# Feature-major down products for two expert layers, weighted by broadcast routing rows and added in place

## What is computed

```python
x = x + L0_ffn(L0_cond(x, cond))      # mixtures of experts
x = x + L1_ffn(L1_cond(cond, x))      # L1_cond: a GRU over the 128 time steps
x = x + L2_ffn(L2_cond(x, v, ...))    # L2_cond: low-rank product and gelu
x = x + L3_ffn(L3_cond(x, cond))      # L3_cond: a tanh recurrence; 12 experts, 3 routers
```

```python
h = gelu(x @ W1[e] + b1[e])                   # for every expert e
out = sum_e comb[:, e] * (h @ W2[e] + b2[e])  # comb: two non-zero weights a token
```

## Time and profile before

| what | value |
|---|---|
| time of the runs | 710.54 us median (703.42 to 712.31) |
| profiled execution | 709.84 us, span 708.1 us |
| TensorE matmul (PE) | 660.8 us busy, 93% |
| TensorE weight load (PEld) | 608.8 us, 86% |
| VectorE (DVE) | 384.4 us, 54% |
| ScalarE (ACT) | 279.1 us, 39% |
| GpSimd (POOL) | 45.5 us, 6% |
| granted TensorE clock, mean | 0.964 of full |

### The profile page before, as it was taken

The page is one execution under the profiler, slowest core; times in us unless marked ns, Lnnn a source line. Parts: engine busy times, 40 slices in busy tenths (PEclk is TensorE's granted clock), DMA queues, the critical chain, the costliest instruction groups (busy, mean ns, idle before and its releaser), DMA issues.

```text
span 708.1 us, 12692 instructions
## 1 busy us (share of the span) xinstructions
PE 660.8 (93%) x4762; PEld 608.8 (86%) x4762; DVE 384.4 (54%) x1462; ACT 279.1 (39%) x930; POOL 45.5 (6%) x55
## 2 busy tenths in 40 slices
PE   5789999879999989999999999997999999999997
PEld 5678887778999978999999999997889889888895
DVE  1885757753657454455544651136555554665504
ACT  0284535533664444544454555545422112110010
POOL 3000000000001000000000000000021221221310
PEclk9999989956999999999999999999989999999999
DMA  9960000000000000000000000400000000000000
GB/s 276 391 246 1 1 1 1 2 0 1 1 2 2 1 1 2 1 1 1 1 2 1 1 1 1 151 30 0 1 1 1 5 5 1 5 5 1 7 1 9
DMA packets 18285, 20.62 MB, mean 29 GB/s; under 512 B 2900, under 2 KB 10928, under 8 KB 18224
## 3 DMA queue, kind: packets, MB, share of 16 engines
q1 hardware_dynamic: 14488, 18.76, 7.6%
q10 hardware_dynamic: 3736, 1.04, 0.6%
HBM read 19.28 MB, written 0.52 MB: 28 GB/s over the span
## 4 chain that ended last, share of the span: by engine, by line
PE 78%; DVE 11%; ACT 3%; issue 3%; DVEq 0%
PE Y L1132 29%; PE U L1132 27%; PE HH L1132 8%; PE ZR L1132 7%; PE M L1132 5%; DVE acc_b L645 1%; DVE acc_a L645 1%; DVE fresh L645 1%; PE M L1402 1%; ACT cand L501 1%; DVE h_gru L645 1%; PE U L1253 1%; DVE rh L645 1%; DVE l_up_lo L637 1%; ACT gated L525 1%
## 5 line engine op out<-in xcount | busy, mean ns | idle before, releaser
L1132 PE MATMUL Y<-l_dn,gated 128*128 128x128 f32 x1152 | 163.5, 286 | 3.7 <-DVE acc_a L827 2.1
L1132 PEld LDWEIGHTS Y<-l_dn,gated 128*128 128x128 f32 x1152 | 142.2, 194 | 6.5 <-issue 4.2
L525 ACT ACTIVATE gated<-U,b1T 128x256 f32<-128x256 f32 x256 | 106.5, 471 | 4.1 <-PE U L1132 4.1
L1132 PE MATMUL U<-l_x_hi,l_up_hi 128*128 128x256 f32 x256 | 84.1, 328 | 0.0
L505 ACT ACTIVATE h<-ZR,rnn_b 128x8 f32<-128x8 f32 x128 | 34.2, 267 | 117.4 <-PE ZR L1132 114.3
L1132 PE MATMUL U<-l_x_lo,l_up_hi 128*128 128x256 f32 x256 | 73.1, 285 | 0.0
L1132 PE MATMUL U<-l_x_hi,l_up_lo 128*128 128x256 f32 x256 | 72.9, 285 | 0.0
L501 ACT ACTIVATE cand<-HH 128x8 f32<-128x8 f32 x128 | 22.7, 177 | 122.6 <-PE HH L1132 122.6
L645 DVE SCALAR_TENSOR_TENSOR fresh<-zr_s,cand 128x8 f32<-128x8 f32 x128 | 22.7, 177 | 70.4 <-ACT cand L501 69.4
L1132 PEld LDWEIGHTS HH<-rh,gru_u 128*128 128x128 f32 x256 | 42.4, 199 | 20.4 <-DVE rh L645 19.3
L1132 PE MATMUL U<-scaled_hi,l_up_hi 128*128 128x256 f32 x192 | 58.7, 306 | 0.0
(11 more groups left out here) (270 smaller groups left out, 1265.1 us busy)
## 6 DMA issues: line engine op xcount, KB each, us to landing
w_raw<-L_ffn_W_dram SPq DMA_DIRECT2D x1, 3072.0 KB, 10.9
l_up_raw<-L_ffn_W_dram SPq DMA_DIRECT2D x1, 2048.0 KB, 14.3
l_up_raw<-L_ffn_w_dram SPq DMA_DIRECT2D x1, 2048.0 KB, 19.7
l0f_up<-L_ffn_w_dram SPq DMA_DIRECT2D x1, 768.0 KB, 6.7
l0f_dn<-L_ffn_w_dram SPq DMA_DIRECT2D x1, 768.0 KB, 8.7
x<-x_dram SPq DMA_DIRECT2D x1, 512.0 KB, 4.4
l_up<-L_cond_W1e_dram SPq DMA_DIRECT2D x1, 512.0 KB, 4.3
l_dn<-L_cond_W2e_dram SPq DMA_DIRECT2D x1, 512.0 KB, 5.3
```

The costliest lines, as they stand in the source:

```text
L525: last = nc.scalar.activation(gated[:, n % 4, h * N:(h + 1) * N], U[n % 2][:, h * N:(h + 1) * N], ACT.Gelu, bias=b1T[:, col:col + 1])
L1132: return nc.tensor.matmul(out, lhsT, rhs, start=start, stop=stop, skip_group_check=shared)
```

## The change

The down product of layers 1 and 2 becomes feature-major: a piece of W2 is the stationary operand and a 128x256 half of `gated` the moving one. A unit so has 2 float32 matmuls of 256 columns instead of 4 of 128, and starts when its own gelu is done. The product has features on the partitions, so the weight of a token is now wanted along the columns, the same for all partitions. TensorE makes such rows from `combT` (now float32r, high part in rows 0 to 7, low part in rows 32 to 39) with a one-hot `sel_expert`, two experts ("a pair") at a time, through M; VectorE copies them to `pair_wb`. `add_layer` multiplies and adds straight into x1 or x3; the first expert's product is only copied and is worked in with the second's, since the weights come later. The biases b2 are one matmul into the free half of the second expert's Y bank. `layer_sum` and its additions are gone. `comb_transposed` moves from slot 6 to slot 5 of a stream. The last up matmuls move behind `gru_cand_of`: two of six in A and B, half of the product in C and F. On VectorE `gru_reset` comes before `taken_late`. In layer 3 the high and low part of dwT are stacked in one operand, so that a broadcast is one matmul an expert. The set-up has four more small DMAs on ScalarE's queue (b2 is loaded three times for each of the two layers, for rows 0, 32 and 64) and more memsets on GpSimd, and `sel_expert` is made at the start.

```diff
 def softmax_combine(g, n, comb_to):
...
+                    for col in (0, 32, 64):
+                        last = tt(spread[:, :, col:col + E], grp(sig_a, g, n), over(den, g, n), ALU.mult)
...
+            def take_weights(n):
+                for l, stream in enumerate("AB"):
+                    if unit(n - 5)[:2] == (stream, 0):
+                        m = taken(f"w{l}", unit(n - 5)[2])
+                        own(v.tensor_copy(combT[l][0:72, :], m[0:72, 0:N]))
+                        tt(combT[l][32:40, :], m[32:40, 0:N], combT[l][32:40, :], ALU.subtract).then_inc(m_free, 1)
...
 def add_layer(n):
-                    add_experts(j + 1, j % 2, [(t * D, t, e) for t in range(TILES)], acc, comb_l, e == 0)
+                x, x_in, held = (x1, x3)[l][:, cols], x1[:, cols], x3[:, cols]
+                y = Y[j % 2]
+                dve.wait_ge(y_full, j + 1)
+                if e == 0:
+                    v.tensor_copy(held, y[:, 0:N]).then_inc(y_free, 1)
+                    dve.wait_ge(y_free, j + 1)
+                    return
+                if e == 1:
+                    own(tt(held, held, pair_wb[:, 0:N], ALU.mult))
+                    own(tt(x, x_in, held, ALU.add))
+                    own(tt(x, x, y[:, N:], ALU.add))
+                tt(weighed, y[:, 0:N], pair_wb[:, at(e % 2 * N, N)], ALU.mult).then_inc(y_free, 1)
+                dve.wait_ge(y_free, j + 1)
+                last = tt(x, x, weighed, ALU.add)
...
+            def take_pair(*name):
+                v.tensor_copy(pair_wb[:, :], taken(*name)[:, :]).then_inc(m_free, 1)
+                dve.wait_ge(m_free, m_of(*name) + 1)
+            def first_pair(n):
+                if unit(n - 6)[:2] in (("A", 0), ("B", 0)):
+                    take_pair("pair" + unit(n - 6)[0], unit(n - 6)[2], 0)
+            def later_pair(n):
+                stream, i, k = unit(n - 3)
+                if stream and stream in "AB" and i in (4, 8, 12):
+                    take_pair("pair" + stream, k, i // 4)
...
                 steps = gru_steps(n)
-                taken_late(n - 1)
                 if steps:
                     gru_reset(steps[0])
+                later_pair(n)
+                taken_late(n - 1)
                 finish(n - 1)
...
                 take_w1(n)
+                take_weights(n)
+                first_pair(n)
                 take_sums(n)
...
 def down_layer(n):
-                for q in range(Q):
-                    hid = gated[:, (last_half - 1 + q // 2) % 4, at((q % 2) * N + t * P, P)]
-                    last = mm(Y[j % 2][:, t * D:(t + 1) * D], hid, dn[stream == "B"][:, e, q, :], q == 0, q == Q - 1)
+                for h in range(2):
+                    q = 2 * t + h
+                    last = mm(Y[j % 2][:, 0:N], dn[l][:, e, q, :], gated[:, n % 4, h * N:(h + 1) * N], q == 0, q == Q - 1)
                 if t == 1:
+                    if e == 1:
+                        pe.wait_ge(m_free, m_of(f"w{l}", k) + 1)
+                        last = mm(Y[j % 2][:, N:], b2[l][:, :], combT[l][:, :])
                     last.then_inc(y_full, 1)
...
-            def layer_sum(n):
+            def weights_pair(stream, k, pair):
...
+                for h in range(2):
+                    last = mm(m[:, h * N:(h + 1) * N], sel_expert[:, 2 * pair + h, :], combT[l][:, :])
                 last.then_inc(m_full, 1)
...
 def l3_broadcast(c, j):
-                    for part in range(2):
-                        last = mm((HH, U[1])[j % 2][:, h * N:(h + 1) * N], sel_expert[:, 2 * j + h, :], dwT[part][:, :],
-                                  part == 0, part == 1)
+                    last = mm((HH, U[1])[j % 2][:, h * N:(h + 1) * N], sel_expert[:, 2 * j + h, :], dwT[:, :])
...
                 project(n)
                 for step in steps[:1]:
                     gru_cand_of(step)
+                project_rest(n)
...
-                layer_sum(n)
                 l2_pre(n)
                 comb_transposed(n)
+                later_pair(n)
                 down(n - 2)
...
                 transpose_w2(n)
+                first_pair(n)
+                transpose_w1(n)
```

More of the change, by code:

```diff
@@ L74 @@
 DOWNS = [n for n, u in enumerate(UNITS) if fills_y(u)]
+X_DONE = [u[::2] for u in UNITS if u[0] in "AB" and u[1] == LU - 1]
 def gru_steps(n):
@@ L102, in x_mid @@
     names = [(name, unit(n - lag)[2]) for name, lag, place in (
[L103 to L104 removed]
+        ("c", 4, ("C", 5)), ("f", 4, ("F", 5)), ("logits", 5, ("C", 5)),
+        ("w0", 5, ("A", 0)), ("w1", 5, ("B", 0))) if unit(n - lag)[:2] == place]
+    stream, i, k = unit(n - 2)
+    names += [("pair" + stream, k, i // 4)] if stream and stream in "AB" and i in (4, 8, 12) else []
     return names
@@ L207, in adaln_ffn_program @@
         x1 = sb("x1", [P, T * B])
+        pair_bias, gru_c = x1[0:40, 0:4 * D], x1[:, 4 * D:7 * D]
         h_gru = sb("h_gru", [P, 2 * N])
+        b2_raw = [h_gru[:, l * D:(l + 1) * D] for l in range(2)]
         l2_in = sb("l2_in", [P, N])
+        with ExitStack() as raw:
+            cond_pair = sb("cond_pair", [40, D], scope=raw)
+            l0f_rw_in = sb("l0f_rw_in", [E, D], scope=raw)
         z1m = sb("z1m", [P, N])
@@ L943, in routing @@
                 for l, stream in enumerate("AB"):
-                    for back in (0, 1, 2, 3, 4, 6):
+                    for back in range(5):
                         if unit(n - back)[:2] != (stream, 0):
@@ L1341, in sums_l0, with first_pair, later_pair @@
                     last.then_inc(m_full, 1)
-            def layer_sum(n):
-                stream, i, k = unit(n - 3)
-                if not stream or stream not in "AB" or i != LU - 1:
-                    return
+            def weights_pair(stream, k, pair):
                 l = int(stream == "B")
-                m = bank(f"sum{l}", k)
-                pe.wait_ge(m_free, m_of(f"w{l}", k) + 1)
-                mm(m[:, 0:N], b2[l][:, :], (combT_a, combT_b)[l][:, :], True, False, True)
-                pe.wait_ge(y_free, DOWNS.index(n - 3) + 1)
-                for t in range(TILES):
-                    last = mm(m[:, t * P:(t + 1) * P], (acc_a, acc_b)[l][:, t, :], ident[:, :], False, True, True)
-                last.then_inc(m_full, 1)
+                m = bank("pair" + stream, k, pair)
+                if (k, pair) == (0, 0):
+                    pe.wait_ge(l3_consts, 1)
+                if pair == 0:
+                    pe.wait_ge(m_free, m_of(f"w{l}", k) + 1)
+                for h in range(2):
+                    last = mm(m[:, h * N:(h + 1) * N], sel_expert[:, 2 * pair + h, :], combT[l][:, :])
+                last.then_inc(m_full, 1)
+            def first_pair(n):
+                stream, i, k = unit(n - 5)
+                if (stream, i) in (("A", 0), ("B", 0)):
+                    weights_pair(stream, k, 0)
+            def later_pair(n):
+                stream, i, k = unit(n - 2)
+                if stream and stream in "AB" and i in (4, 8, 12):
+                    weights_pair(stream, k, i // 4)
             def l2_pre(n):
```

210 lines of the change are left out of this document (119 added, 91 removed).

## The result

The kernel after took 725.69, 732.53, 733.18 and 736.88 us, median 732.86; the kernel before, run beside it, had a median of 706.98. The ratio is 1.032 with an interval of 1.023 to 1.040: the change makes the kernel slower. The forecast was 724.2 with a range of 711 to 738, so the time lies in the range, but above the likeliest case's own 721 to 730. The profiled execution of after is its slowest, 736.88 us (span 735.1), 1.5% above its fastest; what follows keeps apart what every execution shows (the lengths of the slots) from what differs between them (the clock).

The account below looks back on a forecast made before the run. PE's records bound plain slots, VectorE the others. 709.84 + 1.4 - 8.3 (PE's records) + 12.0 + 1.2 + 2.7 + 2.0 = 720.8, plus 3.4 for the clock: 724.2 us, range 711 to 738.

Parts of the forecast that it names:

- likeliest case: Whole kernel: bursts of VectorE and some falls of the clock, 724.2 us, own range 721 to 730, chance 0.40.
- Burst: Slots 6 and 7, six streams: second expert's VectorE copies and five operations make PE wait 2.0 us each, +12.0.
- The rule for W: Slots with a GRU step take the larger of PE's records and W + 1.13; W runs from h to next rh.
- The wait of slot 5: Slot 5, six streams: bias in the down product waits some 0.2 us for combT from VectorE, +1.2.
- Other slots with a pair (11 and 15): Slots 11 and 15: W + 1.4 is 2.4, PE with the pair 2.5, so no cost.
- Down products: Layers 1 and 2: four 256-column records take 0.95 us instead of eight in 0.97; 128 units, -2.6.
- Layer 3's broadcasts: Layer 3 on PE: 48 of 96 broadcast matmuls go, at 0.12 us each, -5.8.
- The start: Set-up: four more DMAs ahead of ScalarE's first activation, +1.4 us; GpSimd's longer set-up up to +1 more.
- two of six: Six slots with a new PE wait: two let the clock fall to half for 3.4 us, +3.4 together.
- rival 3: Clock falls at every burst, some for 6.8 us: 731 to 741 us, chance 0.16.
- Rival 4: PE's records decide after all, VectorE's burst being shorter or hidden: 703 us, chance 0.14.
- rival 5: Weight loads were the price; halving those of A and B takes off up to 99 us: 622 us, chance 0.05.

Follow-up runs that it names:

- b_burst: Kernel before plus useless VectorE work of the burst's size in slots 6 and 7 of the six streams: 720.74 us, ratio 1.022.
- v2: Kernel after with bias and first pair in slot 6, second expert's operations spread over slots 6, 7, 9, later pairs' copies behind h_gru: 714.59 us, ratio 1.011.
- b_pad: Kernel before with the operands of layer 3's broadcasts filled up with zero rows to 128 partitions, no record removed: 703.22 us, ratio 0.990.
- b_stack_third: Kernel before with the change's stacked layer 3 broadcasts, and dwT_third and l3_b2 also filled up to 128 rows: 698.81 us, ratio 0.988.
- b_stack: Kernel before with the change's stacked layer 3 broadcasts alone, one matmul an expert, one-hot columns filled up likewise: 703.24 us, ratio 0.989.

## Why the prediction was right or wrong

**At full clock it was right in sum.** Forecast +11.0 (709.84 to 720.8), measured +10 in span times clock. In part that is luck, a sum of errors of both signs. With half of each stretch at 0.50 taken off, the four stages of the two profiled executions differ by +4.2, +13.3, +2.6 and -10.9 us; the forecast's terms, shared out over the same stages, are +1.4, some +15, some +0.5 and -5.8. By terms:

- Burst: right. The rule for W, spacing (0.45 to 0.47), the copy (0.69), slot 7 of 4.5 (measured 4.62), PE's wait of some 1.7 (1.59). +12.0 was sound: `b_burst` alone gave +8 with a slot 1.64 longer, where after's was 1.7 longer.
- The wait of slot 5, +1.2: right. PE waits 0.27 us between the down product and the bias, 0.2 were forecast. The step into slot 6 is 3.41 against 2.29, but that isn't a miss: the rest of it is transposes that stood one slot later before, and the bias and the pair, which the forecast counted with PE's records (0.36 for them, measured 0.45). Burst, wait, bias and two pairs together were forecast at +2.7 us a stream (2.0 + 0.2 + 0.12 + 0.48, less 4 x 0.02); the four steps of A.2 grew by 2.4.
- "Other slots with a pair (11 and 15): nothing": wrong by some 1.3 us, nine slots of 0.15. They take 2.84 in after and 2.49 in `v2`, where the copy stands behind h_gru, but the slot behind gives 0.20 back (2.05 in after, 2.25 in `v2`). The rule "the larger of the two" failed here. The gates come late, behind the pair's broadcast on PE (2.48 from gates to gates), and VectorE's copy ahead of fresh comes on top of that, since rh waits for these gates and not for VectorE.
- Slots with routing, +2.7: right. The steps that carry it are 0.27 to 0.28 longer, as into A1.2 (2.62, now 2.90), A3.2 (2.70, now 2.98) and B1.2 (2.81, now 3.08).
- Down products: forecast 0.95 for four records, measured 0.86 with an up product ahead and 0.94 with the candidate ahead. The row stands behind an 8-column product, so it had the price of the change in it, which the up product pays now. The forecast of plain slots, 2.27, came out as 2.25.
- Layer 3's broadcasts: -5.8 forecast, -8.5 in span times clock (683 to 674.5) and -11.8 in the stage (-10.9 at full clock). The term was mis-sized, and its parts were others: `b_pad` and `b_stack_third` show some 6 us for the change between 12 and 128 rows, at the broadcasts and at the third router's products, and `b_stack` only 2 for the records themselves. Why these gave 2 and not 5.8 was not tested; the rows around a broadcast, 0.70 and 0.46 us, have the whole 0.24 for two records.
- The start: the +1.4 was right, the first activation stood behind the DMA issues until 17.93 (forecast 17.9). But a term is missing. VectorE now splits b2 into its parts, four operations from 35.42 to 36.53, ahead of work that PE waits for: PE's wait at 39.31 is 1.71 us where it was 0.60. So the first GRU step comes 2.6 us late and not 1.4:

```profile
17.93 1.28 ACT L505 ACT_TABLE_LOAD   x1 [17.93 <-issue]
...
39.31 0.44 PE L1208 MATMUL M<-ident,acc_a 128*128 128x128 f32 x2 [1.71 <-DVE acc_a L656]
```

- The last chunk: forecast +2.0 for VectorE's delays. The stage goes from 112.2 to 114.8 at full clock, +2.6 with PE's records in it. But `b_pad`, in which only the first broadcasts of this stage differ from before, has 114.0 by the same account, so this term can't be told from a smaller one.

**The clock is where it was wrong.** The step that failed is "I take that two of six let the clock fall for 3.4 us: +3.4". Four of six fell, for 10.2, 6.8, 3.4 and 13.7 us, 34 us at 0.50, and over all executions the clock took 14 us more than before. Two things were read too mildly. The trace had three waits of 1.3 to 1.6 us, two with a fall and one without; the forecast went below even those odds. The trace as a whole was nearer to them: it has waits of 1.58 and 1.57 us at 265.59 and 485.28 without a fall and one of 1.35 at 518.24 with one, three of six in all. And the falls that followed were taken to last 3.4 us, although held one of 6.82 and one of 30.72. One of the long ones in after, with PE busy all through:

```profile
436.70:450.40 13.70, 13.70 (x55) 12.62 (x54) 4.08 (x20) 4.29 (x16) 0.00 (x0) 0.50 0.01 1
```

**The rivals.** What came is rival 3 (falls at nearly every burst, some long; 731 to 741), given a chance of 0.16, not the likeliest case. Rival 4 is out by slot 7's 4.62, and rival 5 by the weight loads: 512 of the 1024 loads of A and B went, PEld fell from 608.8 to 597.0 us busy, and the kernel got slower. The Trainium skill (Trainium Kernel Development and Optimization, Best Practices) judges the distance to the roofline by the share of peak arithmetic reached (MFU) and by the busy share of weight loads. Here that share fell from 86% to 81% while the time rose by 3.2%, so it did not tell what bounds this kernel. The chances gave "slower" 0.36 against 0.58 for "within 2%", so the side was missed though the range held.

## What to carry to other kernels

Price the wait that a change creates twice: once for its own length, and once for the clock behind it. Here, in one and the same slot, waits of PE of 1.1 us let the clock fall in none of six places, 1.25 in two of five, 1.6 to 1.7 in eight of eleven and 2.5 to 3.1 in six of six, for 3.4 to 13.7 us; other places had other odds. Where a wait can't be avoided, spread the work behind it over slots with room, or fill it. Products that have to be added cost least in a slot in which PE waits anyway: the bias and the first pair, moved there, gave back 0.73 us a stream, of which only 0.27 had been a wait. And before a long step is called a loss, look whether its neighbour got shorter: work that only moved shows up in one and is missing in the other.

## What the runs showed of the hardware

- A fall of the clock lasts on under full load: 13.7 us at 0.50 with PE busy for all of it (436.70 to 450.40).
- The same wait of PE has different odds at different places: 1.57 to 1.76 us was followed by a fall in two of 16 waits for rh in A.1 outside slot 7, and 1.59 to 1.71 us in eight of eleven slots 7.
- A matmul of 12 rows among ones of 128 costs 0.12 us among its like, and some 0.09 more at each change of the number of rows; zero rows cost nothing. Filling up operands alone made the kernel 1.0% faster (0.986 to 0.995).
- A wide product behind an 8-column one costs 0.08 to 0.09 us more than behind another wide one (float32r 0.20 for 0.12, four float32 records 0.94 for 0.86).
- VectorE's copy of a 128x128 tile within SBUF took 0.23 us before and 1.15 after, where GpSimd's making of `sel_expert` lay beside it:

```profile
10.32 1.55 POOL L465 TENSOR_SCALAR_AFFINE_SELECT sel_expert<-sel_expert 128x1536 fp32r<-128x1536 f32 x1
...
10.80 1.15 DVE L761 COPY cond_tok<-condT 128x128 f32<-128x128 f32 x1
```

The copy ends with GpSimd's operation (11.87 and 11.95). The Trainium skill (SBUF — State Buffer, Who interferes with whom) says that a VectorE instruction in a mode that uses both ports, which a copy can enter, and a GpSimd instruction exclude each other for the whole instruction. The rows agree, but the profile doesn't show the mode, and no run here took GpSimd's work away. It cost nothing, since ScalarE started later still.
